# Loading each block's queries, keys, values and gates through ScalarE's queue instead of SyncE's, and another order in the first block

## What is computed

```python
xn = _layernorm(x)
# attention part: a gated delta rule over 512 tokens, 16 batches x 16 heads, 16x16 state S
q = (h @ Wq) * Dh ** -0.5 ; k = (h @ Wk) / (norm + 1e-6) ; v = h @ Wv      # h = layernorm of xn, with gain and bias
beta = sigmoid(h @ Wb) ; g = sigmoid(h @ Wg)
def step(Sst, inp):
    q_t, k_t, v_t, b_t, g_t = inp
    Sst = Sst * g_t[..., None, None]
    kS = einsum('bhk,bhkv->bhv', k_t, Sst)
    Sst = Sst + b_t[..., None, None] * einsum('bhk,bhv->bhkv', k_t, v_t - kS)
    return Sst, einsum('bhk,bhkv->bhv', q_t, Sst)
x1 = xn + scan(step) @ Wo + bo
attn = x1 + gelu(layernorm(x1) @ w1 + b1) @ w2 + b2
# expert part: 64 experts, top 8, at most 128 tokens each, and a shared expert on all tokens
ffn = segment_sum(silu(xb @ w_gate) * (xb @ w_up) @ w_down * weight) + silu(sg) * su @ ws_down
out = x + attn + ffn
```

## Time and profile before

| | us |
|---|---|
| median of 3 runs (range) | 1885.25 (1883.35 to 1887.22) |
| the profiled execution | 1889.32 |
| its span, first to last instruction | 1887.6 |
| VectorE (DVE) busy | 1692.2 (90%) |
| GpSimd (POOL) busy | 1591.6 (84%) |
| TensorE (PE) busy | 1417.8 (75%) |
| ScalarE (ACT) busy | 813.4 (43%) |

### The profile page before, as it was taken

The page is one execution under the profiler, slowest core; times in us unless marked ns, Lnnn a source line. Parts: engine busy times, 40 slices in busy tenths (PEclk is TensorE's granted clock), DMA queues, the critical chain, the costliest instruction groups (busy, mean ns, idle before and its releaser), DMA issues. The chain is left out here.

```text
span 1887.6 us, 31473 instructions
## 1 busy us (share of the span) xinstructions
PE 1417.8 (75%) x8846; PEld 1235.2 (65%) x8846; DVE 1692.2 (90%) x4987; ACT 813.4 (43%) x2548; POOL 1591.6 (84%) x1353
## 2 busy tenths in 40 slices
PE   6777777877764677566565658898888989988869
PEld 5666666766653566455554647777777877777657
DVE  3599999999999999899977987999899999999980
ACT  4534444545444544345432245444544444434313
POOL 5279999899998889788887788998899899999861
PEclk9978778878875788787877679998999999899878
DMA  8574334533346666856658421242123311111110
GB/s 187 146 179 114 75 99 118 139 83 97 95 124 152 166 149 159 214 116 152 163 135 229 88 54 50 68 131 83 56 58 109 90 53 53 65 50 58 42 50 18
DMA packets 337169, 201.24 MB, mean 107 GB/s; under 512 B 208226, under 2 KB 327716, under 8 KB 336996
## 3 DMA queue, kind: packets, MB, share of 16 engines
q1 hardware_dynamic: 318724, 168.43, 34.3%
q0 software_dynamic: 15616, 30.55, 7.3%
q10 hardware_dynamic: 2656, 0.26, 0.1%
HBM read 127.58 MB, written 71.60 MB: 106 GB/s over the span
## 5 line engine op out<-in xcount | busy, mean ns | idle before, releaser
L823 POOL TENSOR_TENSOR rp<-S,qs 128x2048 f32<-128x2048 f32 x113 | 521.2, 4612 | 44.6 <-DVE S L1144 30.5
L1144 DVE SCALAR_TENSOR_TENSOR S<-S,gwin,bank 128x256 f32<-128x256 f32 x1024 | 481.0, 470 | 0.3
L1134 DVE TENSOR_REDUCE nu<-vwin 128x16 f32<-128x272 f32 x1024 | 435.9, 426 | 0.3
L1138 DVE TENSOR_TENSOR bank<-nu,bank 128x256 f32<-128x256 f32 x1024 | 428.6, 419 | 0.6
L1129 DVE TENSOR_TENSOR vwin<-S,bank 128x256 f32<-128x256 f32 x1024 | 419.7, 410 | 0.3 <-DVE nu L1134 0.2
L831 POOL TENSOR_TENSOR r<-rp 128x1024 f32<-128x1024 f32 x113 | 273.5, 2420 | 7.0
L1792 PE MATMUL bank<-region 128*128 128x128 f32 x2048 | 278.0, 294 | 0.0
L1792 PEld LDWEIGHTS bank<-region 128*128 128x128 f32 x2048 | 262.2, 207 | 18.3 <-issue 17.8
L1672 PE MATMUL bank<-xaT,wqkvg 128*128 128x128 f32 (+1 forms) x1792 | 237.8, 285 | 11.9 <-ACT xaT L1326 8.5
L1803 PE MATMUL bank<-region 128*128 128x256 f32 x1024 | 234.8, 383 | 0.0
L1672 PEld LDWEIGHTS bank<-xaT,wqkvg 128*128 128x128 f32 (+1 forms) x1792 | 212.4, 187 | 26.4 <-ACT xaT L1326 12.6
(11 more groups left out here) (170 smaller groups left out, 2275.0 us busy)
## 6 DMA issues: line engine op xcount, KB each, us to landing
qkv_d<-stg SPq DMA_DIRECT2D x192, 128.0 KB, 3.0
region<-in_L_ffn_w_gate SPq DMA_DIRECT2D x64, 192.0 KB, 4.5
region<-in_L_ffn_w_up SPq DMA_DIRECT2D x64, 192.0 KB, 4.9
region<-in_L_ffn_w_down SPq DMA_DIRECT2D x64, 192.0 KB, 5.9
region<-in_L_attn_x SPq DMA_DIRECT2D x16, 512.0 KB, 7.2
region<-in_L_attn_x SPq DMA_DIRECT2D x32, 256.0 KB, 4.4
xw_d<-region SPq DMA_DIRECT2D x32, 256.0 KB, 3.4
acc_d<-region SPq DMA_DIRECT2D x32, 256.0 KB, 4.2
```

The costliest lines, as they stand in the source:

```text
L823: g.tensor_tensor(rp[:, :, :].rearrange("p (a v) d -> p a v d", v=DH), S[h][:, lo:lo + HS].rearrange("p t s (v d) -> p (t s) v d", v=DH), ...
L1134: m[G] = mark(v.tensor_reduce(nu[:, G], products_of(I, s, G)[1], AX.X, ALU.add))
L1138: m[G] = mark(v.tensor_tensor(outer[G].rearrange("p (v d) -> p v d", v=DH), nu[:, G].unsqueeze(2).to_broadcast([P, DH, DH]), key(L, s, G), ...
L1144: ins = v.scalar_tensor_tensor(S[h][:, s, G], earlier(h, s, G), gwin[:, I // NB2 & 1, G, 1, t:t + 1], outer[G], ALU.mult, ALU.subtract)
```

## The change

1. `next_window` moves from SyncE's program to ScalarE's, with the same waits, and issues the same five loads on ScalarE's queue. In route iterations it stands after `route_out(q, 0, h)` and before `unit_silu(q + 2, 2)`, in expert iterations after `expert_out(n * RT, 0, hx)` and before the same silu, in back iterations behind the first MLP tile's `back_norm` and before `front_qk`, and where there is no MLP tile (iterations 0 and 17) ahead of `front_evac`.
2. For block 0, still on GpSimd's queue, each group's load is keys, gates, values, each with a semaphore of its own; both groups' queries come last.
3. `key_norms(0)` waits for the gates alone, not for whole windows.
4. The values of block 0: VectorE scales the first 8 tokens of both groups (128x16x8 each), GpSimd the other 56 tokens of both (it had the 64 tokens of group 0). VectorE waits for GpSimd's part only at iteration 1.

```diff
-            def next_window(k, s):
-
-                sp.wait_ge(act_staged, k * NB2)
-                sp.wait_ge(rec_done, k * NB2 * 2 + 2)
...
-                window_loads(sp, k + 1, (k + 1) & 1, s)
...
-                    if j < 2:
-                        next_window(I // NB2, j)
                     front_store(f, f // NB2, f % NB2, h)
...
+        def first_keys_load(queue, s):
+
+            queue.dma_start(win[1][:, 0, s], qkv_ld[0, 1, s]).then_inc(first_key[s], 16)
+            for w in range(2):
+                queue.dma_start(gwin[:, 0, s, w], gat_ld[0, s, w]).then_inc(first_gate[s], 16)
+            queue.dma_start(vwin[:, 0, s, :, DH:DH + BLK], qkv_ld[0, 2, s]).then_inc(first_val[s], 16)
+
+        def first_queries_load(queue, s):
+
+            queue.dma_start(win[0][:, 0, s], qkv_ld[0, 0, s]).then_inc(first_win[s], 16)
...
             def scale_values(k, s):
 
-                vw = vwin[:, k & 1, s, :, DH:DH + BLK]
+                lo = 0 if k else ST
+                vw = vwin[:, k & 1, s, :, DH + lo:DH + BLK]
...
-                dve.wait_ge(*window_in(0, 1))
-                vw = vwin[:, 0, 1, :, DH:DH + BLK]
+                for s in range(2):
+                    dve.wait_ge(*values_in(0, s))
+                    vw = vwin[:, 0, s, :, DH:DH + ST]
+                    mark(v.tensor_tensor(vw, vw, rk[:, s, 0:ST].unsqueeze(1).to_broadcast([P, DH, ST]), ALU.mult))
...
+            def next_window(I):
+
+                k, s = I // NB2, I % NB2
+                if s > 1 or k + 1 == NBLK:
+                    return
+                act.wait_ge(rec_done, k * NB2 * 2 + 2)
+                act.wait_ge(act_staged, k * NB2)
+                for at in (window_in, values_in, gates_in):
+                    act.wait_ge(*at(k, s))
+                act.wait_ge(vals_ready, (k + 1) * 3)
+                for i in range(BUF):
+                    act.wait_ge(f_stored[i], (min((k + 1) * NB2 + s, NT - NB2) + 1 - i) // 2 * FST)
+                window_loads(a_, k + 1, (k + 1) & 1, s)
...
                 route_out(q, 0, h)
+                next_window(it)
                 unit_silu(q + 2, 2)
...
+                if not tiles:
+                    next_window(I)
                 if I < R0 or R1 <= I < X0:
                     front_evac(f, h)
```

More of the change, by code:

```diff
@@ L362, in layer @@
         first_key = [sem(f"first_key{s}") for s in range(2)]; first_win = [sem(f"first_win{s}") for s in range(2)]
+        first_gate = [sem(f"first_gate{s}") for s in range(2)]; first_val = [sem(f"first_val{s}") for s in range(2)]
         first_st = [[sem(f"first_st{s}{i}") for i in range(BUF)] for s in range(2)]
@@ L466, in window_in, with values_in, gates_in @@
         def window_in(k, s):
-            return (win_ld[s], k * WLD) if k else (first_win[s], WLD)
+            return (win_ld[s], k * WLD) if k else (first_win[s], 16)
+        def values_in(k, s):
+            return (win_ld[s], k * WLD) if k else (first_val[s], 16)
+        def gates_in(k, s):
+            return (win_ld[s], k * WLD) if k else (first_gate[s], 32)
+        def first_keys_load(queue, s):
[5 more added lines that the diff above has]
+            queue.dma_start(win[0][:, 0, s], qkv_ld[0, 0, s]).then_inc(first_win[s], 16)
         def window_loads(queue, k, par, s):
-            key_in, rest_in = keys_in(k, s)[0], window_in(k, s)[0]
+            key_in, rest_in = key_ld[s], win_ld[s]
             queue.dma_start(win[1][:, par, s], qkv_ld[k, 1, s]).then_inc(key_in, 16)
@@ L787, in _ @@
                 pool.sem_inc(passed, 1)
-                window_loads(pool, 0, 0, s)
+                first_keys_load(pool, s)
+            for s in range(2):
+                first_queries_load(pool, s)
             def square_sums(k, s):
@@ L870, in _ @@
             pool.wait_ge(sv_ready, 1)
-            scale_values(0, 0)
+            for s in range(2):
+                pool.wait_ge(*values_in(0, s))
+                scale_values(0, s)
             def residual(I):
@@ L1216, in first_scales @@
                 dve.sem_inc(sv_ready, 1)
-                dve.wait_ge(*window_in(0, 1))
-                vw = vwin[:, 0, 1, :, DH:DH + BLK]
-                v.tensor_tensor(vw, vw, rk[:, 1, :].unsqueeze(1).to_broadcast([P, DH, BLK]), ALU.mult).then_inc(vals_ready, 1)
+                for s in range(2):
+                    dve.wait_ge(*values_in(0, s))
+                    vw = vwin[:, 0, s, :, DH:DH + ST]
+                    mark(v.tensor_tensor(vw, vw, rk[:, s, 0:ST].unsqueeze(1).to_broadcast([P, DH, ST]), ALU.mult))
                 link(v.tensor_tensor(first_groot[:, :, 1], first_groot[:, :, 0], first_groot[:, :, 1], ALU.mult))
@@ L1234, in body @@
                 j = I % NB2
+                if I == 1:
+                    dve.wait_ge(vals_ready, 3)
                 dve.wait_ge(prod_done, I * 2)
@@ L1265, in _ @@
             for k in range(NBLK):
-                dve.wait_ge(vals_ready, (k + 1) * 3)
+                if k:
+                    dve.wait_ge(vals_ready, (k + 1) * 3)
                 for s in range(2):
                     dve.wait_ge(*keys_in(k, s))
-                for s in range(2):
-                    dve.wait_ge(*window_in(k, s))
+                    dve.wait_ge(*values_in(k, s))
+                    dve.wait_ge(*gates_in(k, s))
                 stage_factors(k)
@@ L1589, in back_iteration @@
                         back_norm(i + 2)
+                    if p == 0:
+                        next_window(I)
                     if f is not None and p == 0:
```

12 lines of the change are left out of this document (3 added, 9 removed).

## The result

The changed kernel took 1919.98 us (median of 4 runs, 1919.74 to 1920.21), the kernel before 1886.13 beside it. The ratio is 1.0181, with a 95% interval of 1.0167 to 1.0194: 33.9 us slower. The forecast was 1904.5, so the direction was right and the size was not. The profiled execution took 1920.15 us, 30.8 more than that of before (1889.32).

What follows compares the result with a forecast made beforehand. VectorE's recurrence was taken to bound the kernel. Terms 5.7 + 3.2 + 3.0 + 3.7 + 3.7 + 0 + 4.8 - 4.8 = 19.3 us, added to the median 1885.25, gave 1904.5 us; range 1877 to 1920.

Steps and rivals of the forecast that it cites:

- What bounds: Whole kernel: VectorE's recurrence sets the end; edits count by its idle time; ScalarE at most some 1 to 3 us ahead.
- B = 5.5: Time in us that one window load's five issues hold ScalarE, taken from SyncE's iteration 9; ends 2.1 and 10.8.
- my longest, 10.8: Upper end in us for one window load's holding, with the gates at 9.29; as a rival 1935 us, chance 0.08.
- The first rival: ScalarE's queue hardly held, row loads and the scatters of iterations 25 and 33 faster: 1874 us, chance 0.2.
- Part 1: Before iteration 0: VectorE's first token 4.5 us earlier (2.8 to 6.9), a gain not kept.
- the bound of 4.1: Before iteration 0: VectorE's small scalings wait for both GpSimd scalings, 2.07 us each, leaving a lead of 2.8.
- Part 2: Iteration 0: load ahead of front 16 waits for front 15's store, then holds ScalarE; first silu at 112.9, +5.7 us.
- Parts 2 and 3: Iterations 0 and 1: loads delay the first silu and that of r = 2, +5.7 and +3.2 us, 8.9 together.
- Part 4, iterations 8 and 9: Silus 3.7 us later, less slack of 1.04 at r = 2 in iteration 9: +3.0 us for both iterations together.
- Part 4, iterations 16 and 17: Late silu in 16, load ahead of front 33 and the counts in 17: +3.7 us each.
- Part 5: Expert iterations 24, 25, 32, 33: late silus hidden behind VectorE's waits for GpSimd's products, 0; otherwise 2 to 3 us each.
- Part 6: Back iterations 40, 41, 48, 49: late gelus +4.8 us, SyncE's relief at TensorE's row wait -4.8.

Runs made afterwards that it cites:

- the opening alone: Changed kernel's opening (queries last, split scalings) with all 14 window loads back on SyncE at their old places; 1884.67 us, ratio 0.9988 to the kernel before.
- the pair alone: Changed kernel with only the window loads of iterations 8 and 9 on ScalarE, the other twelve on SyncE; 1894.24 us, ratio 1.0020 to the kernel before.
- the back alone: Changed kernel with only the window loads of iterations 40, 41, 48 and 49 on ScalarE; 1890.39 us, ratio 1.0006 to the kernel before.

## Why the prediction was right or wrong

**What bounds.** Right. The change pays or costs by VectorE's idle time, and ScalarE, busy 43%, sets it through the chain with TensorE.

**B = 5.5.** The mechanism was right, the size a little low: 6.4 on average, 6.9 and 8.2 in iterations 9 and 8. I took B from one window. The same view of the kernel before shows SyncE held 4.7 to 13.0 us, 7.8 on average over the 14 windows, and 5.48 is the second shortest; my longest, 10.8, was not the longest either. That the gates wait for the values ahead of them was shown by moving the values. The first rival (hardly held, 1874) is dead. Of its other half, the scatters beside the window loads, at most a little is true: GpSimd's wait for the one in iteration 33 is 3.04 us instead of 4.95 (5.31 with the opening alone); that in iteration 25 is 2.46 instead of 3.63, but 2.44 with the opening alone too.

**Part 1.** VectorE's first token came at 72.17, 4.25 earlier (4.5 forecast), with the two scalings ending only with GpSimd's (4.29 us), as the bound of 4.1 had it. With that bound the sum gave 2.8; the rest came from ScalarE's `key_norms`, 5.15 us earlier (61.02) and not 3.80, as ScalarE's own work ahead of it was 1.2 us earlier in this execution. So 4.5 was close in part by luck. The reading of 3.44 - 2.36 = 1.08 as VectorE's own share is borne out: alone, two such scalings take 2.36 us. The lead was not kept, as forecast.

**Part 2.** ScalarE's load began at 90.00, not 93.3, and its `xaT` came at 96.75 (98.8 forecast); the hold was 6.65. The silu ended at 111.95 (112.9), and VectorE's product came at 111.98 behind 8.94 us of idle time. Parts 2 and 3 together: 8.9 forecast over the kernel before; the start of iteration 2 is +6.5. Right in kind, 2.4 too high.

**Part 4, iterations 8 and 9: the step that failed.** "I put iterations 8 and 9 at +3.0 together, since the next iteration's rows come by a load whose waits absorb part." The changed kernel lost 12.0 there, and the pair alone 10.7. Three things were wrong. First, I charged one silu per load with hold less slack, and left out the next silu: the stall comes again at r = 3, as the chain from silu to silu takes 4.9 us where VectorE needs 3.2, and TensorE, idle for 5.2 to 5.9 us in the run of the pair, runs the next matmuls at half its clock, some 2 us more. The slack of 1.04 that I used for iteration 9 is that of r = 2; at r = 3 there was none in the kernel before, VectorE already waited:

```profile
354.69 0.42 DVE L1069 TENSOR_TENSOR hg_s<-sgu,bank 96x256 f32<-96x256 f32 x1 [0.71 <-ACT sgu L1418]
```

In iteration 8 the slack was 3.40 us at r = 2 and 1.59 at r = 3. Counted at r = 3, the last silu of the iteration, the cost comes out of two numbers: in iteration 8 that silu is 9.1 us later in the iteration than before, 9.1 - 1.6 = 7.5, and VectorE's next start moves by 7.5; in iteration 9 it is 4.4 later, with no slack, and the start moves by 4.4. Second, B: the holds here were 8.2 and 6.9 us. Third, nothing was absorbed: the wait for the rows of the next iteration is ScalarE's, and it does not give VectorE any time back. As stalls, the 12.0 are 3.86 + 3.50 in iteration 8 and 2.25 + 3.87 in iteration 9, less the 1.8 that VectorE waited for silus in iteration 9 before.

**Part 4, iterations 16 and 17.** 7.4 forecast, 6.4 measured (20.6 to 27.0). The sum was right by chance: all of it came in iteration 16, again by two stalls, and none in 17.

**Part 5.** 0 was right in the main: from iteration 24 to 34 the delay even falls by 2.2 us. VectorE does stall at silus there (1.38 us in iteration 25, 3.6 in 33), but its waits for GpSimd's products shrink by more, from 8.5 to 5.2 us in iteration 25 and from 10.4 to 6.2 in 33 (30.9 to 23.3 in all).

**Part 6.** 0 forecast. The delay grows by 6.8 from iteration 40 to 43 and is 4.1 above that of 40 in iteration 48; the back alone measured +3.4. SyncE's relief came as forecast: TensorE's wait of 4.78 us for rows is gone in both runs, and 4.5 us come back in iteration 43. But the holds cost more than 1.2 each: VectorE waits 4.87 us in iteration 41 and 1.65 in 42 for TensorE, where it did not before.

Against the forecast of 19.3, 14.6 us are missing. By the table: iterations 8 and 9 +9.0, from iteration 40 to the end +8.4 (25.15 to 33.53, where 0 was forecast; 1.7 of it, at iteration 60, is also in the trace of the pair (1.6), which has no load of ScalarE's there), iterations 0 and 1 -2.0, 16 and 17 -1.0, and -0.2 in small steps elsewhere (+1.7 from 10 to 16, +1.4 from 18 to 24, -3.3 from 24 to 40). That is 14.2, from one execution of each kernel.

## What to carry to other kernels

An engine that issues a DMA is held until its queue takes it, and a tiny transfer behind one of many small pieces can hold it far longer than its bytes: put the transfer of many pieces last, with no other DMA close behind it on that queue, and issue from an engine whose stream nobody waits for. Read the hold from all windows of a trace, not from one. Where a compute engine must choose the moment, let it signal and another issue. When costing a delay in a chain of two engines, count every link that VectorE takes from it, not just the first, take the slack at the last one, and look at what TensorE's clock does behind the gap.

## What was unexpected of the hardware

One 512 KB transfer in front decided what the next ones cost their issuer: on ScalarE's queue two gates took 2.9 to 6.5 us behind the values and 0.9 to 1.6 ahead of them; on SyncE's, ahead of them, 0.9 in most windows. Issuing the values took only 0.53 to 0.66 us in the first case and mostly 0.53 to 0.84 in the second: the price falls on whoever comes behind, on SyncE's queue the next store (6.08 us instead of 1.67). The keys, also 512 KB, hold nobody: the gates right behind them are the ones of 0.9 to 1.6. By the shapes of the rows the keys are 128 rows of 4 KB and the values 128 x 16 pieces of 256 bytes; that the pieces make the difference is the likely reason, and no run varied them alone.

VectorE took 2.36 us for 2 x 1024 elements a row with GpSimd idle, and 4.29 us for 2 x 128 while GpSimd worked on the same kind of operation for 4.14. A small share of VectorE's work beside GpSimd's can be dearer than all of it alone.
